# Two layers of a transformer on one core: the first maximum products made twice, a third slot for q's pieces, narrower token products, and a new written order

## The reference

```
xn = layernorm(x)
x  = x + attention0(xn) + mixture0(xn)   # 32 query heads of 16, ONE key/value head, causal, alibi; LoRA mixture: top 2 of 4 experts
xn = layernorm(x)
x  = x + attention1(xn) + ffn1(xn)       # attention1: per token a 16x16 softmax; ffn1: silu(gate)*up, down, 512 -> 1792 -> 512
```

## Time and profile before

| | |
|---|---|
| median of 3 runs | 619.19 us (618.67 to 620.34) |
| the profiled execution's own time | 620.43 us |
| its span | 618.4 us |
| TensorE | 584.1 us busy (94%) |
| VectorE | 464.0 us (75%) |
| ScalarE | 384.1 us (62%) |
| GpSimd | 368.2 us (60%) |
| mean granted TensorE clock | 0.97 |

### The profile page before, as it was taken

How to read it: one execution, slowest core, us unless ns; L and a number is a source line. 1 busy time by engine, 2 the same in 40 slices (tenths; PEclk the granted TensorE clock), 3 DMA queues, 4 the chain that set the end, 5 groups by cost and what they waited for, 6 DMA issues and landing times.

```text
span 618.4 us, 14499 instructions
## 1 busy us (share of the span) xinstructions
PE 584.1 (94%) x5689; PEld 427.9 (69%) x5689; DVE 464.0 (75%) x1041; ACT 384.1 (62%) x707; POOL 368.2 (60%) x378
## 2 busy tenths in 40 slices
PE   4989797799989999999999999999999999999997
PEld 3755553467866568786868687876786787779763
DVE  6878886899999848988887569969982774676541
ACT  5485576677875567776766657866665777624310
POOL 6146946765676744875559537865667578524321
PEclk9978897599999999999999999999999999999999
DMA  7125898803574048001920330026001200000000
GB/s 164 45 77 116 198 248 130 110 2 54 56 120 88 0 87 108 2 3 21 87 37 2 42 68 2 2 31 112 2 2 38 69 1 1 32 6 1 1 35 34
DMA packets 79495, 34.49 MB, mean 56 GB/s; under 512 B 55916, under 2 KB 70604, under 8 KB 79364
## 3 DMA queue, kind: packets, MB, share of 16 engines
q1 hardware_dynamic: 73236, 25.14, 23.4%
q0 software_dynamic: 2352, 7.18, 5.6%
q10 hardware_dynamic: 3840, 1.26, 1.1%
HBM read 28.58 MB, written 7.34 MB: 58 GB/s over the span
## 4 chain that ended last, share of the span: by engine, by line
PE 83%; DVE 9%; ACT 4%; issue 2%; SPq 1%; POOL 1%; DMA 1%; ACTq 0%; DVEq 0%
PE B_bank L1349 29%; PE B_bank L1370 15%; PE A_bank L1302 8%; PE E_bank L1255 7%; PE A_bank L1275 6%; PE B_bank L1227 4%; PE A_bank L1193 4%; SPq L763 1%; PE A_bank L1144 1%; PE A_bank L1186 1%; PE A_bank L1286 1%; PE B_bank L1186 1%; PE B_bank L1337 1%; PE A_bank L1126 1%; PE E_bank L1259 1%
## 5 line engine op out<-in xcount | busy, mean ns | idle before, releaser
L943 POOL TENSOR_TENSOR probs<-e,probs 128x512 f16<-128x512 f32 x192 | 229.3, 1204 | 103.3 <-ACT probs L1063 103.0
L1349 PE MATMUL B_bank<-xs,wgu 128*128 128x256 f16 x1792 | 208.3, 273 | 3.0 <-DVE hf L1750 3.0
L1349 PEld LDWEIGHTS B_bank<-xs,wgu 128*128 128x128 f16 x1792 | 173.9, 98 | 27.6 <-DVE hf L1750 3.3
L1062 ACT ACTIVATE e<-E_bank,wn 128x512 f32<-128x512 f32 x192 | 132.5, 690 | 75.2 <-PE E_bank L1255 49.2
L1063 ACT ACTIVATE probs<-E_bank,wn 128x512 f16<-128x512 f32 x192 | 132.7, 691 | 0.0
L957 POOL TENSOR_TENSOR hbuf<-hf,hbuf 128x512 f16<-128x512 f32 x56 | 65.8, 1179 | 81.0 <-ACT hbuf L1101 80.9
L1370 PE MATMUL B_bank<-wd,hbuf 128*128 128x512 f16 x448 | 103.2, 379 | 0.0
L1643 DVE TENSOR_REDUCE mx<-B_bank 128x2 f32<-128x448 f32 (+10 forms) x179 | 94.5, 575 | 6.8 <-PE B_bank L1227 6.4
L1111 ACT ACTIVATE ebuf<-B_bank,sgx 128x256 f32<-128x256 f32 x112 | 46.8, 477 | 53.1 <-PE B_bank L1349 52.8
L1255 PE MATMUL E_bank<-qq,kk 128*128 128x256 f16 (+1 forms) x320 | 73.2, 305 | 6.7 <-ACT probs L1063 5.9
L1370 PEld LDWEIGHTS B_bank<-wd,hbuf 128*128 128x128 f16 x448 | 43.1, 98 | 44.6
(11 more groups left out here) (216 smaller groups left out, 677.4 us busy)
## 6 DMA issues: line engine op xcount, KB each, us to landing
x<-in_x SPq DMA_DIRECT2D x20, 256.0 KB, 5.5
qq<-q_parts SPq DMA_DIRECT2D x18, 256.0 KB
out_y<-x SPq DMA_DIRECT2D x16, 256.0 KB, 2.2
xa<-in_x SPq DMA_DIRECT2D x12, 256.0 KB, 3.6
q_parts<-qs SPq DMA_DIRECT2D x48, 64.0 KB, 3.3
wgu<-in_gate_w POOLq DMA_DIRECT2D x4, 448.0 KB, 9.8
wgu<-in_up_w POOLq DMA_DIRECT2D x4, 448.0 KB, 11.8
wd<-in_down_w POOLq DMA_DIRECT2D x4, 448.0 KB, 7.3
```

What stands on the lines that cost most here:

```text
L943: pool.tensor_tensor(probs[:, u % PSLOTS, 1, :], e32[:, w, :], probs[:, u % PSLOTS, 0, :], ALU.subtract).then_inc(s_lop, 1)
L1062: act.activation(e32[:, w, :], psum("exp", i, g, w)[:, :], ACT.Exp, scale=wn[:, 7:8])
L1349: mm = pe.matmul(psum(name, u, i)[:, a * SEQ:(a + 1) * SEQ].rearrange("p (t n) -> p t n", t=NU), wgu[:, m, k, (2 * i + a) * P:(2 * i + a + ...
```

## The change

Five things. `passes(i)` is 2 for batches 0 and 1: each of their maximum products is issued twice, back to back, with the same operands into the same place, so its value is unchanged. `qs` has three slots instead of two. `tok1` multiplies the low part of its tokens with two of the three parts of the weights instead of all three: 96 columns instead of 144 for half of its products (the third part times the low part is left out). Two costs of the planner are other numbers. And all five lists of QUEUES are written anew.

```
+QSLOTS = 3
+WARMED, PASSES = 2, 2
...
+def passes(i):
+
+    return PASSES if i < WARMED else 1
...
-             "q": 1.3, "pv": 0.62, "attT": 0.46, "midT": 0.13, "outa": 1.3, "out": 1.74, "xT1": 0.46, "tok1": 1.0,
+             "q": 1.3, "pv": 0.62, "attT": 0.46, "midT": 0.13, "outa": 1.3, "out": 1.74, "xT1": 0.46, "tok1": 0.85,
...
-        xT0*2 tok norm q0 norm2 xT0*2 q0 tok q0 kT max*4 kT max*12 q0 max*2 nm0 q0 max*2 exp max*3 exp max exp q0 exp*2
+        xT0*2 tok norm xT0*2 q0*2 norm2 tok q0 kT*2 max*16 q0 max*3 nm0 q0 max*2 exp max*3 exp*2 q0 exp*2 q0 exp*2 pv
...
-        return 0.01 + count * max(0.03, GT * (tb + 1) / 2400)
+        return 0.01 + count * passes(step[1]) * max(0.03, GT * (tb + 1) / 2400)
...
-            end[e, step] = free[e] = t + cost(e, step) * (1.15 if e == "PE" and 25 < t < 110 else 1.0)
+            end[e, step] = free[e] = t + cost(e, step) * (1.05 if e == "PE" and 25 < t < 125 else 1.0)
...
-        p.add("ACT", ("q", c, m), pe("q", c, m), *([sp("q", (n - 2) // NK, (n - 2) % NK)] if n - 2 >= NK else []))
+        p.add("ACT", ("q", c, m), pe("q", c, m), *([sp("q", (n - QSLOTS) // NK, (n - QSLOTS) % NK)] if n - QSLOTS >= NK else []))
...
-        qs = sb("qs", [P, 2, 2, CHUNK], F16)
+        qs = sb("qs", [P, QSLOTS, 2, CHUNK], F16)
...
-                    store_heads(sp, c, b, m, qs[:, m % 2, :, b * SEQ:(b + 1) * SEQ], s_qd[m])
+                    store_heads(sp, c, b, m, qs[:, (c * NK + m) % QSLOTS, :, b * SEQ:(b + 1) * SEQ], s_qd[m])
...
-                if n - 2 >= NK:
-                    act.wait_ge(s_qd[(n - 2) % NK], 16 * 2 * NB * ((n - 2) // NK))
+                if n - QSLOTS >= NK:
+                    act.wait_ge(s_qd[(n - QSLOTS) % NK], 16 * 2 * NB * ((n - QSLOTS) // NK))
...
-                for g in range(count):
+                for g in [g for g in range(count) for _ in range(passes(i))]:
...
-                        for part in (0, 1):
-                            mm = pe.matmul(psum("tok1", u)[:, t * 3 * C1:(t + 1) * 3 * C1],
+                        for part in (0, 1) if k < NK - 1 else (1, 0):
+                            parts = 3 - part
+                            mm = pe.matmul(psum("tok1", u)[:, 3 * t * C1:(3 * t + parts) * C1],
                                            xs[:, (NU * u + t) % NT, part, k, :],
-                                           w48[:, k, :, :].rearrange("p a n -> p (a n)"),
-                                           start=(k == 0 and part == 0), stop=(k == NK - 1 and part == 1))
+                                           w48[:, k, 0:parts, :].rearrange("p a n -> p (a n)"),
+                                           start=(k == 0 and part == 0), stop=(k == NK - 1 and part == 0), skip_group_check=True)
```

More of the change, by code:

```diff
@@ L127 @@
[L127 to L141, removed]
@@ new lines @@
+        max*2 exp*2 q0 exp*2 pv*2 exp xT0*2 max midT pv tok max*3 xT0*2 max*7 nm0 norm2 tok exp*2 max qa*2 exp*2 q*2
+        max*2 exp pv qa q cmax qa max*4 q max*3 exp max*2 exp max exp max*2 exp max pv nmT exp*3 kT pv exp*2 pv exp
+        attT*2 exp*3 xT0*2 exp max*4 xT0 outa out pv max*2 pv exp outa exp*2 out xT0 max*2 exp pv exp max*2 qa q max*2
+        exp max*2 qa max*2 exp*2 xT1 q xT1 exp max qa max exp pv max*2 q max gate exp nmT tok1 exp pv gate exp up exp*2
+        pv up midT exp*2 gate*2 exp*2 pv up*2 exp kT pv gate*2 exp*2 attT*2 up*2 pv exp max*2 exp tok*2 max gate max exp
@@ new lines @@
+        kT exp up*2 attT exp attT exp gate*2 pv tok exp up*2 max exp max*2 tok max*3 exp qa exp q max*4 outa out max exp
+        pv max pv max*3 exp outa exp max exp out exp max*3 gate exp*2 gate max exp up pv*2 up exp max xT1 gate xT1 exp
+        up exp nmT half half2 gate exp pv half3 down exp up tok1 exp*2 pv gate*2 exp*2 half kT pv half2 exp half3 attT*2
+        down exp up midT up pv max exp max*3 exp max outa max*2 exp max*2 out max*4 exp*2 pv outa max*4 exp out max
+        exp*2 max*2 pv gate exp gate exp*2 up pv exp up gate exp*2 pv max gate midT up nmT xT1*2 exp*2 up half exp half2
@@ new lines @@
+        pv exp tok1 gate half3 exp pv exp down kT exp up gate*2 exp pv half attT*2 exp*2 half2 half3 exp down exp max pv
+        max*2 outa max up*2 exp max*2 out exp*2 max*4 pv exp max*2 outa max*2 exp*2 max out pv max*2 exp gate*2 exp*2
+        max up*2 pv xT1 midT xT1 exp max gate max gate exp*2 up max pv exp up exp nmT half pv half2 exp tok1 gate exp*2
+        half3 down exp*2 half half2 pv*2 exp up exp attT gate attT exp*2 half3 exp down pv outa exp*2 out outa exp up
+        exp pv out gate*2 exp up*2 xT1 exp gate exp pv midT gate up exp xT1 gate up*2 gate exp pv exp half tok1 half2
@@ L146 @@
+        exp pv up half3 down exp half exp*2 half2 exp pv half3 exp*2 gate exp pv down gate*2 pv up attT*2 up*2 outa*2
+        out*2 gate up gate xT1 up xT1 gate up gate*2 tok1 up*2 half half2 gate*2 half3 down half half2 half3 down up*2
+        gate up gate*2 up*2 half half2 half3 down half half2 half3 down
         """,
     "ACT": """
[L148 to L149 removed]
@@ L159 @@
         """,
     "DVE": """
[L161 to L164, removed]
@@ new lines @@
+        scale2 tok place q0 place max*16 place max*2 q0 nm0 max*3 q0 max*3 place mix ln0 q0 mixb q0 pv ln0*3 q0 place
+        max pv*2 xn0*4 xT0*2 max place*2 pv tok max*4 place max*3 xT0*2 norm2 nm0 max*2 tok scale2 setup0 max*3 q*2 pv
+        max*5 cmax q max*3 q max*7 ln0 nmT ln0*2 pv setup1 xn0 pv*2 xn0 setup3 attT*2 xn0 xT0*2 max*4 xT0 ln0 out pv*2
+        xn0 max ln1 max out xT0 max*3 pv max ln1 max*3 xn1*2 max*2 q max q xT1*2 max*5 q pv tok1 nmT att1 gate pv gate
+        pv att2 up*2 mix att3 gate pv gate up*2 att4 pv mixb attT*2 gate*2 pv max up*2 max*2 tok max tok gate max*4 pv q
```

82 lines of the change are left out of this document (40 added, 42 removed).

## The result

The changed kernel takes 625.31 us in the median of 4 runs (624.24 to 626.96), the kernel before 619.77 beside it: ratio 1.0086 (95% interval 1.0052 to 1.012). It is slower by 0.9%, and outside the range. Measured again with 12 runs (experiment 8) it was 624.21, ratio 1.0045 (1.0018 to 1.0073). The profiled execution took 626.96 us, its span is 625.0, against 618.4 before.

A forecast was written before the change was run, and what follows sets the result against it. TensorE's own work was taken to bound the kernel from about 123 us, a chain of waits before. Gather's issue -0.5, its landing -2.0 and `tok1` -1.3 sum to -3.8: 615.4 us for the median, range 608 to 621.5.

The forecast's parts named there:

- the gather's landing: `gather(2)`, at 112 to 122 us: with the x loads gone from there it lands 2.0 us earlier.
- The new order behind 123 us I count as nothing.: In TensorE's full stretch the rewritten orders change nothing: 0 us, as TensorE idles only 3.2 us from 140 to 200.
- `setup0`: VectorE waits for `su` from 76.5 to 85.6 us; TensorE stands about 8 us; q's low halves come 2.0 later.
- the quick stores: SP's first eight q stores come after POOL's weight loads and so run faster: -2.5 us.
- the load of chunk 2: SP's load waits for `q(1, 3)`, claimed done at 96.2 us, before SP gets there at 97.3: no delay.
- third rival: TensorE at 1.2 GHz behind the `setup0` stall delays `q(1, 3)` and the gather by 7.2 us: 622.6 us, chance 0.16.
- The clock early: Around 42 and 56 us doubled products keep TensorE at 2.4 GHz; with an exp reordered, -5.3 us to the last `q0(1, m)`.
- x loads: Moved ahead of q's stores, they push back POOL's weight loads, and so `su`'s landing, by 2.0 us.
- Third slot: ScalarE's 2.85 us wait for a store gains nothing when removed, since SP's queue is busy throughout: 0.
- `tok1`: 64 of 128 products lose 48 columns each, in full TensorE time: -1.3 us.
- predicted front -2.5, rear -1.3: Before the full stretch, -0.5 for the gather's issue and -2.0 for its landing; in TensorE's full stretch, -1.3 for `tok1`.

The follow-up runs named there:

- experiment 8: The changed kernel itself measured once more, with 12 runs: 624.21 us, ratio 1.0045 to the kernel before.
- Experiment 2: From the changed kernel, GpSimd's first two loads of the down weights put back behind `up(0, 3)`: 618.13 us, ratio 0.9953 to the kernel before.
- 9: From the changed kernel, `pv(1, 7)` ahead of `att4(0)` on VectorE alone, GpSimd's order kept: 625.3 us, ratio 1.0057 to the kernel before.
- 5: The changed kernel with `setup0` and `cmax` moved back and GpSimd's two down-weight loads back behind `up(0, 3)`: 613.77 us, ratio 0.9878 to the kernel before.
- Experiment 1: From the changed kernel, `setup0` back behind the eleventh maximum of batch 1 on VectorE, `cmax` following on both engines: 619.88 us, ratio 0.999 to the kernel before.
- 6: The changed kernel with `setup0`, `cmax` and GpSimd's two down-weight loads moved back, and one maximum pass: 612.52 us, ratio 0.9885 to the kernel before.
- experiment 4: The kernel before with only the second pass of the maximum products of batches 0 and 1 added: 622.59 us, ratio 1.0026 to the kernel before.
- experiment 10: From the changed kernel, the three x loads for the feed-forward back behind `gather(2)`: 624.17 us, ratio 1.0057 to the kernel before.
- experiment 11: The kernel before with three slots for q's pieces instead of two, its own orders kept: 621.93 us, ratio 1.0015 to the kernel before.
- experiment 7: The kernel before with the shorter `tok1` products alone: 619.43 us, ratio 0.9974 to the kernel before.
- experiment 12: The kernel before with GpSimd's exps moved ahead of `up(0, 2)` and down-weight loads later, nothing else changed: 618.5 us, ratio 0.9963 to the kernel before.
- experiments 1, 3: 3: the changed kernel with the maximum products of batches 0 and 1 made once, not twice: 622.37 us, ratio 1.004 to the kernel before.

## Why the prediction was wrong

Two steps failed. One was not seen at all, one was seen and put among the rivals. A third term, the gather's landing, was too large.

**"The new order behind 123 us I count as nothing."** Of the single terms this one has the largest error. I bounded it by the 3.2 us that TensorE idled in that stretch; but that bounds only what a better order can bring, not what a worse one can cost. In the two profiled executions it cost 3.6 us in the rear, 4.9 with `tok1`'s 1.3 set against it; beside the other two rears of the old order (493.3, 494.7) it is 0.8 to 2.2, and without the hole the new order would have been some 4 us ahead. The stall came from a wait on another engine: GpSimd's loads, moved ahead of two `up` and the exps beside them, wait for `gather(3)` with work queued behind them, and while GpSimd worked that off, VectorE's small operation did not end. Experiment 2 shows that the order of GpSimd is the cause, 9 that the place of `att4(0)` on VectorE is not, 5 that it is separate from the first hole.

**`setup0`.** The mechanism was right: predicted a wait of VectorE from 76.5 to 85.6, q's first low half done at 89.8, a hole of about 8 us; found 80.8 to 87.62 (to 86.42 in the second profile), 92.2, and 5.89. What was wrong is where it ended. I let SP catch up, -2.5 for the quick stores. They gave 5.1 (4.87 us for 9.98), more than the later start of 4.4 cost. But I took the load of chunk 2 as not late, done with `q(1, 3)` at 96.2 against 97.3 for SP. It was late: the hole ended at 90.46 and not at 87.9, and TensorE then needed 9.84 us to the end of `q(1, 3)` and not 8.3, being at 1.2 GHz until 93.6. SP stood 3.23 us, to 100.33. So `gather(2)` came 2.62 later and not 0.5 earlier (109.91 to 110.66 in the three profiles with the front of before, 110.86 to 113.28 in the four with the changed one). It is the third rival's path, a late `q(1, 3)`, but not at its price: that rival had all 8.3 us of work at 1.2 GHz. That its 622.6 is the nearest of all to the result is luck, since it knows nothing of the rear. Experiment 1 takes the step back and wins 5.2 to 7.3 us at the landmark.

**The clock early.** The falls at 42 and 56 us went, as predicted, and `q0` takes 1.99 us. `q0(1, 3)` came 3.2 us earlier and not 5.3. But in the new order it was not the doubled products that brought it: with one pass the new order has the same clock from 43 us on and is there 1.24 us sooner. In the old order they bring 0.9 us at that step (59.30 for 60.22) and it is lost behind the gather. Their price was put by the ratios between nothing (5 against 6) and 0.26% (experiment 4).

**`gather(2)`'s landing.** -2.0 predicted. From its issue to `max(2, 0)` it is 10.69 us instead of 12.03, so -1.3. I sized the term by bytes and did not ask how far off the next releaser was. In the chain of before TensorE could have started `max(2, 0)` only 0.99 us sooner:

```profile
121.70 0.99 issue
```

In the changed kernel the DMA engines are nearly idle from 121 us on (share 0.20 and less), and `max(2, 0)` starts at 123.97. The chain that ended last passes over VectorE's list (the reduction of `setup1` in it), then batch 1's `attT`, exps and `xT0`, and not over the gather:

```profile
111.22 2.21 DVE ebuf L1629
...
116.49 1.96 PE A_bank L1293 x8
...
123.97 1.44 PE B_bank L1234 x24
```

From `max(2, 0)` to the landmark it is then 5.55 us instead of 3.82, with TensorE at 0.50 until 127.4; in the second profile it is 4.23.

**x loads.** +2.0 on `su` predicted; 0.2 to 2.3 found by one profile of experiment 10, which is not distinct from nothing, and nothing at the end. **Third slot.** 0 predicted, no gain shown (experiment 11). **`tok1`.** -1.3 predicted, 1.6 measured, with an interval that touches none (experiment 7).

In sum for the profiled execution: predicted front -2.5, rear -1.3; found front +3.0, rear +3.6. By the means of all profiles with the same front it is +1.4 in the front, and the second measurement of the whole is +2.9.

What stays open: the changed kernel's two measurements differ by 0.4%; and of experiment 5's 1.2% over before, 0.26% are `tok1` and 0.37% the hole of experiment 12 (7.5 minus 1.6 and 2.3, so some 3.6 us remain). Between 1.6 and 3.4 of these lie in the front (landmark 124.05, against 125.68 to 127.43); which of the moves there earns them was not tried one by one. Nor was it tried why the clock rises at different times in kernels with the same orders.

## What to carry to other kernels

When a change rewrites an order, look on every engine for a step that waits on a transfer and has moved ahead of ready work: `su` on VectorE and `gather(3)` on GpSimd cost 3 to 6 and 6 to 8 us by the ratios of experiments 1 and 2, while the change without these two moves was 1.2% faster than before. TensorE's idle time in a full stretch bounds what order can win there, never what it can lose. An earlier start is worth only what the clock lets through: the 1.9 us by which `max(2, 0)` came earlier in experiment 4 were gone at the landmark, with TensorE at 1.2 GHz. And before a term is taken from one releaser, look how far off the next one is: behind the gather it was 1 us. Last, a difference of 1 or 2 us between two single profiles can be chance: kernels with the same front differed by 3.2 us here.

## What the hardware showed

A small operation of VectorE stood still through a whole run of GpSimd's: 128x32 numbers took 5.57 to 6.09 us in six profiles (the changed kernel twice, experiments 1, 3, 9 and 10) and 0.28 us in experiments 2 and 5. In the changed kernel it ended at 179.49, GpSimd's fifth operation at 179.43; in experiment 9, where a sixth followed without a pause, at 179.45 and the sixth at 179.39. The Trainium skill (SBUF — State Buffer, Who interferes with whom) states that VectorE and GpSimd share a pair of ports as an exclusive lock, and that a two-input operation on SBUF contends with GpSimd's reads there. The traces fit this, and add a length: the wait lasted as long as the whole run of five or six operations, not as long as one. That it was this lock, and which port, no run here shows.

TensorE's clock did not follow the length of an idle row alone: behind 3.04 us in the kernel before, the stage 172 to 200 us had 1.00; behind 3.03 us in experiment 4 and 3.05 in experiment 11, the next sixteen products took 3.32 and 3.59 us and not 1.92. By stage, before first, then experiments 4 and 11:

```profile
178.20:181.10 2.90, 2.90 (x67) 2.78 (x66) 2.85 (x8) 0.63 (x1) 0.05 (x1) 1.00 1.05 197
178.20:181.10 2.90, 2.88 (x14) 2.02 (x15) 2.88 (x6) 0.00 (x0) 0.48 (x1) 0.50 0.94 155
178.20:184.30 6.10, 5.97 (x63) 4.92 (x64) 3.82 (x10) 0.63 (x1) 2.87 (x3) 0.50 1.02 192
```

An estimate from these rows: 2.9 and 6.1 us at half the clock lose 1.4 and 3.0 us, and the rears, whose order is the same, are 1.4 and 2.8 us longer than that of before.
